# A loop over rounds written out on TensorE, and two input loads moved within SyncE's queue

## The reference, cut to what matters

```
# x: [64 samples, 64 tokens, 1024]; 4096 tokens in all
def L0(x, W, condition):                    # layer 0
    y = einsum('bct,bcd->bdt', x, W[condition])   # mix 64 tokens of a sample, W is 64x64
    base  = y @ W_base.T + b_base                 # 1024 x 1024
    route = top2_softmax(y @ W_gate.T)            # 8 experts
    h     = (y @ A.T) * route                     # rank 16 each, 8 experts: 128 columns
    return base + h @ B
x = x + L0(x)
def L1(x, weight, adapter_ids):             # layer 1
    c     = x @ weight[adapter_id].T              # 1024 x 1024 per sample
    low   = c @ A.T                               # 128 columns
    score = 8 * softmax(c @ Wr.T + br)
    return 2 * (low * score) @ B
x = x + L1(x)
```

## Time and profile before

| | |
|---|---|
| median of 3 runs | 749.4 us (748.09 to 749.75) |
| the profiled execution | 748.57 us |
| its span, first to last instruction | 746.9 us (1.7 us lie around it) |
| PE busy | 724.3 us, 97% |
| DVE, ACT, POOL busy | 335.3, 114.1, 57.8 us |
| mean granted TensorE clock | 0.992 |
| adapter loads, issue to landing | 5.1 / 7.1 / 15.7 us (least, median, most) |

### The profile page before, as it was taken

The page is one execution under the profiler, slowest core; times in us unless marked ns, Lnnn a source line. Parts: engine busy times, 40 slices in busy tenths (PEclk is TensorE's granted clock), DMA queues, the critical chain, the costliest instruction groups (busy, mean ns, idle before and its releaser), DMA issues.

```text
span 746.9 us, 12572 instructions
## 1 busy us (share of the span) xinstructions
PE 724.3 (97%) x4502; PEld 647.4 (87%) x4502; DVE 335.3 (45%) x887; ACT 114.1 (15%) x309; POOL 57.8 (8%) x115
## 2 busy tenths in 40 slices
PE   7999899999999999999999999998999999999996
PEld 7999887898888888888889888787889888998996
DVE  2000196136534644354535563464427552574644
ACT  1222300111111111111111111111111211120111
POOL 1222300001100010001000110000000100010100
PEclk9999999999999999999999999999999999999998
DMA  7999993037721883159504871277415951476552
GB/s 262 340 417 365 392 403 119 1 117 294 250 80 63 295 315 125 56 181 394 195 29 176 314 286 48 86 259 279 173 57 183 405 179 57 168 301 236 208 192 72
DMA packets 38709, 156.31 MB, mean 209 GB/s; under 512 B 8836, under 2 KB 11908, under 8 KB 28420
## 3 DMA queue, kind: packets, MB, share of 16 engines
q1 hardware_dynamic: 27714, 78.72, 28.4%
q0 software_dynamic: 9216, 71.31, 25.9%
q10 hardware_dynamic: 1730, 5.58, 1.9%
HBM read 133.24 MB, written 22.35 MB: 208 GB/s over the span
## 4 chain that ended last, share of the span: by engine, by line
PE 81%; issue 8%; DVE 4%; DMA 4%; POOL 2%; ACT 0%; POOLq 0%; ACTq 0%; DVEq 0%
PE base_ps L333 16%; PE base_ps L334 16%; PE base_ps L335 16%; PE mix_both L353 7%; DMA adapter<-folded 4%; PE low_ps L401 4%; PE out_ps L401 4%; PE mix_both L366 3%; PE base_ps L342 2%; POOL adapter L943 2%; PE out_ps L333 2%; PE out_ps L334 2%; PE out_ps L335 2%; DVE w_lo L683 1%; PE low_ps L366 1%
## 5 line engine op out<-in xcount | busy, mean ns | idle before, releaser
L333 PE MATMUL base_ps<-yT,w_hi 128*128 128x512 f32 (+1 forms) x576 | 214.7, 373 | 1.3 <-DVE xT L803 1.1
L335 PE MATMUL base_ps<-yT,w_hi 128*128 128x512 f32 (+1 forms) x576 | 211.5, 367 | 0.0
L334 PE MATMUL base_ps<-yT,w_lo 128*128 128x512 f32 (+1 forms) x576 | 211.3, 367 | 0.0
L687 DVE TENSOR_TENSOR yT<-mix_both,yT 128x512 fp32r<-128x512 f32 x64 | 44.2, 691 | 240.9 <-ACT yT L560 240.9
L333 PEld LDWEIGHTS base_ps<-yT,w_hi 128*128 128x128 f32 x576 | 108.5, 188 | 20.8 <-DVE xT L803 4.0
L335 PEld LDWEIGHTS base_ps<-yT,w_hi 128*128 128x128 f32 x576 | 108.4, 188 | 18.1
L334 PEld LDWEIGHTS base_ps<-yT,w_lo 128*128 128x128 f32 x576 | 108.6, 189 | 15.4
L342 PE MATMUL base_ps<-ag_raw,stage 128*128 128x136 f32 x640 | 76.0, 283 | 2.2 <-issue 2.2
L342 PEld LDWEIGHTS base_ps<-ag_raw,stage 128*128 128x128 f32 x640 | 75.9, 193 | 2.4 <-issue 2.4
L957 POOL DMA_DIRECT2D adapter<-folded x60 | 31.9, 532 | 576.5 <-PE low_ps L401 503.8
L699 DVE TENSOR_TENSOR x1T<-xT,x1T 128x256 fp32r<-128x256 f32 x120 | 45.3, 420 | 65.1 <-ACT x1T L567 65.1
(11 more groups left out here) (150 smaller groups left out, 747.3 us busy)
## 6 DMA issues: line engine op xcount, KB each, us to landing
adapter<-folded POOLq DMA_DIRECT2D x63, 1088.0 KB, 7.1
stage<-in_w SPq DMA_DIRECT2D x40, 512.0 KB, 8.0
x_rows<-in_x SPq DMA_DIRECT2D x32, 512.0 KB, 6.0
xT<-in_x_turned SPq DMA_DIRECT2D x16, 1024.0 KB, 7.5
out<-xT SPq DMA_DIRECT2D x28, 512.0 KB, 2.7
folded<-adapter ACTq DMA_DIRECT2D x10, 544.0 KB, 6.7
w_raw<-in_w SPq DMA_DIRECT2D x8, 256.0 KB, 8.0
w_raw<-in_w SPq DMA_DIRECT2D x4, 512.0 KB, 12.1
```

What stands on the lines that cost most here:

```text
L333: pe.matmul(dst, st_hi, mv_lo, start=start, stop=False, skip_group_check=True)
L334: pe.matmul(dst, st_lo, mv_hi, start=False, stop=False, skip_group_check=True)
L335: return pe.matmul(dst, st_hi, mv_hi, start=False, stop=stop, skip_group_check=True)
L687: dve.tensor_tensor(yT[:, 1, k, :], mix_ps[k % 2][:, :], yT[:, 0, k, :], ALU.subtract).then_inc(yT_lo_done, 1)
```

## The change

TensorE's rounds 1 to 6 are written out in its program; the other four engines keep their loops. SyncE loads x not whole at the start of a round but in four pieces of 256 columns (two k), for the round after next, each when the two steps of `mix` that read these columns are done, which is in the second half, ahead of the store with the same number. xT(r + 1) is loaded behind the stores of round r - 1, which free its halves, and ahead of the eight small DMAs of the next iteration. A piece is one DMA of 512 KB in runs of 1 KB. `mix` waits for a piece at k = 0, 2, 4 and 6 in place of one wait at k = 0. Ahead of the rounds xT(0) and the pieces of x(1) are loaded, and SyncE's loop has one pass fewer (rounds 1 to 4), with rounds 5 to 7 written out.

```diff
--- before.py
+++ after.py
@@ -169,6 +169,7 @@
         side_lo = sem("side_lo")
 
         x_landed = sem("x_landed")
+        x_pair_landed = [sem(f"x_pair_landed{p}") for p in range(KC // 2)]
         wc_landed = sem("wc_landed")
         xT_landed = [sem(f"xT_landed{h}") for h in range(4)]
         stored = [sem(f"stored{h}") for h in range(4)]
@@ -253,6 +254,13 @@
                     sp.dma_start(x_rows[:, t, :], x[bass.ds(at(q, r, TILES, t), 1), :, :].rearrange("a p n -> (a p) n")
                                  ).then_inc(x_landed, 16)
 
+            def load_x_columns(q, r, pair):
+
+                cols = slice(2 * pair * P, (2 * pair + 2) * P)
+                sp.wait_ge(yT_done, at(q, r - 1, KC, 2 * pair + 2))
+                sp.dma_start(x_rows[:, :, cols], x[bass.ds(at(q, r, TILES), TILES), :, cols].rearrange("t p n -> p t n")
+                             ).then_inc(x_pair_landed[pair], 16)
+
             def load_wc(q, r):
                 for i in range(PER):
                     no = sp.value_load(ids[0:1, bass.ds(at(q, r, PER, i), 1)], min_val=0, max_val=CONDS - 1)
@@ -278,17 +286,18 @@
                 sp.dma_start(out[bass.ds(at(q, r, 4, pair), 1), :, :, toks].rearrange("a p k n -> (a p) k n"),
                              xT[:, h, two, toks]).then_inc(stored[h], 16)
 
-            def iteration(q, r, l0=True, l1=True, ahead=True):
+            def iteration(q, r, l1=True, ahead=True, x_ahead=True):
                 if ahead:
                     sp.wait_ge(yT_done, at(q, r + 1, KC))
-                    load_x(q, r + 1)
                     load_wc(q, r + 1)
-                if l0:
-                    load_xT(q, r, 0)
-                    load_xT(q, r, 1)
-                if l1:
-                    for pair in range(4):
+                for pair in range(4):
+                    if x_ahead:
+                        load_x_columns(q, r + 2, pair)
+                    if l1:
                         store_out(q, r - 1, pair)
+                if ahead:
+                    load_xT(q, r + 1, 0)
+                    load_xT(q, r + 1, 1)
 
             sp.dma_start(ids[:, SAMPLES:], adapter_ids).then_inc(ids_landed, 16)
             sp.dma_start(ag1_raw[:, :, :].rearrange("p k n -> p (k n)"), ag1).then_inc(ag1_landed, 16)
@@ -315,11 +324,17 @@
 
             for p in range(2):
                 sp.wait_ge(folded_stored[p], 16 * total)
+            load_xT(0, 0, 0)
+            load_xT(0, 0, 1)
+            for pair in range(4):
+                load_x_columns(0, 1, pair)
             iteration(0, 0, l1=False)
-            with sp.Fori(0, (ROUNDS - 2) // 2) as q:
+            with sp.Fori(0, (ROUNDS - 4) // 2) as q:
                 for r in (1, 2):
                     iteration(q, r)
-            iteration(0, ROUNDS - 1, ahead=False)
+            iteration(0, ROUNDS - 3)
+            iteration(0, ROUNDS - 2, x_ahead=False)
+            iteration(0, ROUNDS - 1, ahead=False, x_ahead=False)
             for toks in (A, B):
                 for pair in range(4):
                     store_out(0, ROUNDS - 1, pair, toks)
@@ -345,8 +360,11 @@
 
             def mix(q, r, k):
                 if k == 0:
-                    pe.wait_ge(x_landed, at(q, r, 16 * TILES, 16 * TILES))
+                    if isinstance(q, int) and r == 0:
+                        pe.wait_ge(x_landed, 16 * TILES)
                     pe.wait_ge(wc_landed, at(q, r, 16 * PER, 16 * PER))
+                if k % 2 == 0 and not (isinstance(q, int) and r == 0):
+                    pe.wait_ge(x_pair_landed[k // 2], at(q, r, 16))
                 if k >= 2:
                     pe.wait_ge(yT_lo_done, at(q, r, KC, k - 1))
                 for t in range(TILES):
@@ -496,10 +514,9 @@
                 mix(0, 0, k)
             iteration(0, 0, l1=False)
             pe.wait_ge(side_lo, SIDES)
-            with pe.Fori(0, (ROUNDS - 2) // 2) as q:
-                for r in (1, 2):
-                    iteration(q, r)
             last = ROUNDS - 1
+            for r in range(1, last):
+                iteration(0, r)
             iteration(0, last, ahead=False, toks=A)
 
             for k in range(KC):
```

## The result

The changed kernel takes 738.59 us (median of four runs, 737.89 to 739.38) against 748.9 us before. The ratio is 0.9868, 95% interval 0.9845 to 0.9891: 1.3% or 10.3 us faster. The forecast was 739.6 us, within 738.0 to 744.0.

A forecast was written before the change was run, and what follows sets the result against it. TensorE, busy 97% of the span, was taken as the bound; 3.41 (jumps) + 1.70 (slow clock) + 4.23 (late adapters) = 9.34 off 748.57 gives 739.2, adjusted towards the median to 739.6 us, range 738.0 to 744.0.

The forecast's parts named there:

- The account of the 9.34 us: Rounds 2 to 6 on TensorE: 403.39 us, 9.34 more than five times round 1's floor of 78.81, all to be saved.
- The jumps and the clock, 3.41 + 1.70: Ends of rounds 2 and 4: two loop jumps stop TensorE for 3.41 us; half clock behind the first loses 1.70.
- The late adapters, 4.23: First halves of rounds 2 to 6: adapters late behind xT loads in a full DMA queue; all cured, 4.23 us.
- the two terms simply add: Rounds 2 to 6: savings from TensorE without its loop (3.41 + 1.70) and from the queue (4.23) summed to 9.34 us.
- x in pieces: Second half of a round: column pieces of x, 4.8 us per 512 KB in an empty queue, cost TensorE's path 0.
- start where they did: SyncE's eight small loads: still begin about 5 us into a round, 10.16 us to issue, needed at 44 us.
- The start and the tail: Ahead of the rounds, xT(0) asked for earlier costs 0, at most 5.0 us; round 7 and tail unchanged, nothing taken.
- B: Rival, chance 0.13: adapters stay late, in these rounds or others; only 5.11 us saved, 743.5 us.
- C: Rival, chance 0.10: one or two fetch stops left in the written out rounds, perhaps with slow clock; 740.6 to 742.9 us.
- E: Rival, chance 0.03: slower, straight code fetched late on full DMA engines; six stops eat the 9.34, twelve give 759.6 us.
- D: Rival, chance 0.04: the stop belongs to every second round's end, not the jump; only the queue's part saved, 744.3 us.
- F: Rival, chance 0.03: another engine's jump comes to light; a 2.00 us stop costs 0, one of 5 us gives 744.6.

The follow-up runs named there:

- e1_pe_only: The kernel before with only TensorE's rounds written out, SyncE's queue as before the change: 741.73 us, ratio 0.9917 to before.
- e3_one_jump: The changed kernel with TensorE's rounds 1 to 4 in a loop of two passes, 5 and 6 written out (one jump back): 740.8 us, ratio 0.9888.
- e2_queue_only: The changed kernel with TensorE's loop put back, so only SyncE's queue differs from the kernel before: 742.24 us, ratio 0.992 to before.
- e6_xT_moved: e1_pe_only with xT moved behind the stores as in the change, x still whole at the round's start: 738.5 us, ratio 0.9858 to before.
- e12_xT_at_15_but_last: The changed kernel, SyncE written out, xT loaded about 15.3 us into its round except round 7's, which stays behind round 5's stores: 741.3 us, ratio 0.9899.
- e4_all_out: The changed kernel with SyncE's, ScalarE's, VectorE's and GpSimd's rounds written out too: 739.15 us, ratio 0.9872 to before.

## Why the prediction was right, point by point

**The account of the 9.34 us** was right as a total: rounds 2 to 6 gave back 9.39 us. Cutting at the rounds and taking the best round as floor did this; five rounds fell onto it.

**The jumps and the clock, 3.41 + 1.70.** The mechanism is shown: the stop goes where the jump goes (e1_pe_only, e3_one_jump) and stays when only the queue changes (e2_queue_only), and it ends 1.5 to 1.6 us behind the landing of a block of TensorE's program. The sizes: in e2_queue_only's trace the rounds with jumps and those behind them cost 5.3 us, close to the 5.11, but by another mix, with a second stop and no slow clock. That the numbers agree is luck. By the times it is 742.24 - 739.15 = 3.1 us, both on one chip; the slow clock came behind two jumps of five, so a term of one execution is not the mean.

**The late adapters, 4.23.** The mechanism (xT's 2 MB among the adapter loads) is shown by e6_xT_moved and e12_xT_at_15_but_last. The term was over-sized as a cost of its own: without the jumps it is 1.9 us in the rounds of e1_pe_only's trace, and 741.73 - 739.15 = 2.6 us by the times.

**That the two terms simply add** is the step that failed. In rounds 2 to 6 of the traces TensorE alone gave back 7.5 us (forecast: 5.11) and the queue alone 4.1 (forecast: 4.23), in all 11.6, but both together 9.4. By the times, on one chip, TensorE alone saved 7.3 us and the queue alone 6.8, in all 14.1, but a kernel with both (e4_all_out) 9.9. That is a surplus of 4.2 us, uncertain by 2 or more; the 2.2 us of the rounds are the better figure, since round 7 and the tail differ by 1 to 2 us between traces of equal code. So some 2 to 4 us were there only as long as jumps and badly placed loads were there together; each half of the change could claim them. The sum did not suffer, since it was taken from an execution that had both. What joins them is open: round 5 before, with its adapter of 11.60 us, stands behind a jump, and a jump shifts SyncE's loads by 1 to 2 us against TensorE's steps; no run isolates that.

**x in pieces.** Nothing on TensorE's path, as taken; nothing gained either. That the eight small loads "start where they did" held in the rounds and not at the start, where they came 15 us later and 9 us before their use.

**The start and the tail** at nothing: 0.33 and 0.1 us. The first is within what the other traces showed (round 1 began at 160.5 to 161.9 us in them). The second is luck, as shown above: later adapters in round 7 cost 1.3 us and the clock, which did not fall at the end, gave 1.5 back.

**The rivals.** B (adapters stay late) is excluded for rounds 1 to 6. C and E (fetch stops in straight code): TensorE has no idle time with "issue" in rounds 1 to 6, also with all five engines written out, though its program came in 32 blocks. D is excluded by e3_one_jump. F is excluded as far as e4_all_out can tell: 739.15 against 738.59 us.

The Trainium skill's page "Runtime: NRT & Kernel Launch", section "Instruction fetch mechanics", has a taken branch out of the fetched window wait for a DMA fetch. The traces agree: the stops of 1.4 to 2.0 us at the jumps, and in e2_queue_only 0.3 and 1.0 once more, each end 1.2 to 1.6 us behind the landing of a block of queue q8. The page's rule is for each engine. Here only TensorE's jumps cost time (e4_all_out); that the others' hide in their waits is the likely reason, but no trace was read for it.

## What to carry to other kernels

Cut the trace at the rounds of a loop, take the best as floor, and explain each excess: two rounds in six that are longer by 1.4 to 2 us with "issue" at their end are the loop's own jump. Write out the loop of the engine that bounds first; here the loops of the other four cost nothing that shows. Put large loads without a deadline where the queue is empty, away from small ones with a deadline, and add slack (one slot more) where a chain of loads runs at the rate of the DMA engines. Of terms read from one execution trust the sum more than the parts: stops and late loads can be the same microseconds. Compare single traces by the windows that the change touches: their ends can differ by more than the effect.

## What the runs showed of the hardware

- A jump back of TensorE's program fetches two or three more blocks of 16 KB (queue q8: 37 blocks with two jumps, 35 with one, 32 with none) and stops TensorE for 1.4 to 2.0 us (five jumps in three traces); matmuls go on 1.5 to 1.6 us behind the landing of a block.
- Behind both jumps of e2_queue_only, and behind none of the other three, a second stop came 3.1 us after the restart: 0.15 and 0.86 us of idle time (0.31 and 1.03 us from start to start over the usual).
- In rounds 1 to 6 the granted clock fell to its lower level (0.50) behind idle times of 1.85 and 1.73 us (before, e3_one_jump) and stayed at 1.00 behind 1.25, 1.42, 1.83 and 2.17 us (before, e2_queue_only). It cost 1.7 us each time.
- In round 7 it was at 0.50 behind waits of 3.61 and 4.07 us: eight matmuls took 2.17 us in place of 1.16. Behind shorter waits (0.65 to 1.3 us) such a group took 1.27 at 1.00.
- In the last 24 matmuls, between short waits for VectorE, it fell in nine traces of fourteen: 4.3 to 4.6 us in place of 3.1.
- The same 2 MB load cost TensorE nothing when asked for 2 us into a round, about 1 us in all at 12 to 14, 2 to 3 us at 15.3 and 0.5 us at 23. The adapters' median landing was 5.3 to 5.5 us with the load at 2 us (5.6 to 5.9 with x whole), 7.0 to 7.3 at 12 to 15.3 and 5.4 at 23.
- On DMA engines at a share of 1.05, four loads of 512 KB in runs of 1 KB took 19.06 us to issue; four in runs of 4 KB had taken 1.77 us at 1.06.
